# Attention and a spline FFN on one core: the copy of the FFN's constants in four parts in the second batch, and the fourth value tile projected before the first head

## The reference

```python
def reference(x, Wq, bq, Wk, bk, Wv, bv, Wo, bo, gate_cp, up_cp, down_cp):   # x: (4, 512, 512)
    xn = layernorm(x)
    # attention, 16 heads of 32
    q, k, v = (heads(xn @ W + b) for W, b in ((Wq, bq), (Wk, bk), (Wv, bv)))
    scores = q @ k.T / sqrt(32) + slope[h] * distance        # causal mask
    attention = merge(softmax(scores) @ v) @ Wo + bo
    # FFN, 512 -> 2048 -> 512; its weights are made from control points
    gate_w, up_w, down_w = (spline_reconstruct(cp) for cp in (gate_cp, up_cp, down_cp))
    ffn = (silu(xn @ gate_w.T) * (xn @ up_w.T)) @ down_w.T
    return x + attention + ffn
```

## Time and profile before

| | |
|---|---|
| Median of three executions | 844.9 us |
| The profiled execution: its time | 845.87 us |
| Its span (first to last instruction) | 844.1 us |
| Mean granted clock of TensorE | 0.912 of full speed |
| PE busy | 703.6 us (83%) |
| DVE / ACT / POOL busy | 505.1 / 439.5 / 354.6 us |
| DMA moved | 109.79 MB |

### The profile page before, as it was taken

The page is one execution under the profiler, slowest core; times in us unless marked ns, Lnnn a source line. Parts: engine busy times, 40 slices in busy tenths (PEclk is TensorE's granted clock), DMA queues, the critical chain, the costliest instruction groups (busy, mean ns, idle before and its releaser), DMA issues. The chain is left out here.

```text
span 844.1 us, 14059 instructions
## 1 busy us (share of the span) xinstructions
PE 703.6 (83%) x4884; PEld 558.1 (66%) x4884; DVE 505.1 (60%) x1273; ACT 439.5 (52%) x961; POOL 354.6 (42%) x207
## 2 busy tenths in 40 slices
PE   5677879889789898798898684169895999999997
PEld 4566657667567676576776563147684888888886
DVE  5286687779968888877798767185341321221212
ACT  4267566677748776666778751135441233233221
POOL 2343363445535444634455435145223334434434
PEclk9879689999989999899899798569997999999999
DMA  7982564454585336644545917664617545434401
GB/s 252 207 205 37 101 92 153 58 88 75 114 202 76 50 69 134 92 153 58 89 73 124 319 74 246 230 212 136 184 23 228 174 148 175 140 92 138 133 1 50
DMA packets 53024, 109.79 MB, mean 130 GB/s; under 512 B 6361, under 2 KB 6617, under 8 KB 51417
## 3 DMA queue, kind: packets, MB, share of 16 engines
q1 hardware_dynamic: 52808, 108.82, 51.6%
q10 hardware_dynamic: 144, 0.07, 0.0%
HBM read 59.32 MB, written 25.17 MB: 100 GB/s over the span
## 5 line engine op out<-in xcount | busy, mean ns | idle before, releaser
L988 POOL TENSOR_TENSOR work<-work 128x1280 f16<-128x1280 f32 x64 | 168.4, 2630 | 228.3 <-DVE work L714 228.1
L901 ACT ACTIVATE work<-work,neg_max 128x128 f32<-128x128 f32 (+3 forms) x256 | 142.2, 564 | 105.5 <-DVE neg_max L706 104.7
L706 DVE CUSTOM_DVE_ANT_0 work<-bank,dist 128x128 f32<-128x128 f32 (+3 forms) x256 | 115.4, 487 | 82.5 <-PE bank L513 68.2
L1476 POOL TENSOR_TENSOR in_lo<-inner,in_hi 128x512 fp32r<-128x512 f32 x64 | 84.0, 1313 | 180.5 <-ACT in_hi L1379 180.5
L1430 DVE TENSOR_TENSOR inner<-bank,silu 128x512 f32<-128x512 f32 x64 | 44.1, 689 | 135.7 <-ACT silu L1373 122.4
L910 ACT COPY work<-bank 128x768 f16<-128x768 f16 (+1 forms) x128 | 110.3, 909 | 28.5 <-PE bank L527 27.2
L527 PE MATMUL bank<-ident,work 128*128 128x128 f16 x1280 | 109.9, 231 | 10.3 <-DVE work L721 8.5
L513 PE MATMUL bank<-k_stack,q_stack 96*128 96x256 f32 (+2 forms) x256 | 81.6, 397 | 41.5 <-issue 22.5
L1379 ACT CAST in_hi<-inner 128x512 fp32r<-128x512 f32 x64 | 39.8, 621 | 146.4 <-PE bank L1318 137.6
L527 PEld LDWEIGHTS bank<-ident,work 128*128 128x128 f16 x1280 | 78.6, 103 | 50.4 <-issue 33.2
L1316 PE MATMUL bank<-w_room,in_hi 128*128 128x512 f32 x256 | 100.9, 394 | 0.4 <-POOL in_lo L1476 0.4
(11 more groups left out here) (101 smaller groups left out, 1429.0 us busy)
## 6 DMA issues: line engine op xcount, KB each, us to landing
q_stack<-parts SPq DMA_DIRECT2D x48, 256.0 KB, 5.6
k_stack<-parts SPq DMA_DIRECT2D x48, 256.0 KB, 5.6
z<-xt_scratch SPq DMA_DIRECT2D x128, 88.0 KB
x_in<-x SPq DMA_DIRECT2D x32, 256.0 KB, 5.7
xt_scratch<-xt_room SPq DMA_DIRECT2D x8, 1024.0 KB, 6.8
xt_room<-xt_scratch SPq DMA_DIRECT2D x6, 1024.0 KB, 8.2
factor<-c_basis SPq DMA_DIRECT2D x5, 1024.0 KB, 9.7
taps<-windows SPq DMA_DIRECT2D x5, 1024.0 KB, 11.6
```

The lines of the kernel that those rows point to most:

```text
L706: dve.tensor_tensor_reduce(probs[:, s % 2, OFF[i]:OFF[i] + n], score_bank[i % 2][:, 0:n], dist[:, S - n:S], -slope(s), 3.4e38, ALU.add, AL ...
L901: e = act.activation(tile, tile, ACT.Exp, bias=neg_max[:, s % 2, i:i + 1], scale=-1.0, accum_out=row_sum[:, s % 4, i:i + 1])
L988: pool.tensor_tensor(probs16[:, s % 2, 1, :], probs[:, s % 2, :], probs16[:, s % 2, 0, :], ALU.subtract).then_inc(lo_ready, 1)
L1476: pool.tensor_tensor(in_lo[:, k % 2, :], inner[:, k % 2, :], in_hi[:, k % 2, :].bitcast(F32), ALU.subtract).then_inc(il_ready, 1)
```

## The change

The copy of the constants becomes four DMAs of 32 rows each. `lay_out(sp, part)` issues one of them, and part 0 the zeros as well. They are issued in the round b = 1 of SP's loop, behind `stack(0, 3)`, `stack(1, 0)`, `stack(1, 1)` and `stack(1, 2)`. The fourth value tile is projected right behind the third, in front of step 0, and DVE takes all four tiles there; in the list `PJ_FIRST`, `("v", 3)` and `("q", 1)` change places.

```diff
-            sp.wait_ge(bases_st, 16)
+            sp.wait_ge(bases_st, 64)
...
-        def lay_out(sp):
-            sp.dma_start(bases_d, c_bases[:, 0:BM_COLS + BD_COLS]).then_inc(bases_st, 16)
+        def lay_out(sp, part):
+            rows = slice(part * P // 4, (part + 1) * P // 4)
+            sp.dma_start(bases_d[rows], c_bases[rows, 0:BM_COLS + BD_COLS]).then_inc(bases_st, 16)
+            if part:
+                return
...
-PJ_FIRST = [("x", t) for t in range(QT)] + [("q", 0), ("k", 0), ("v", 0), ("v", 1), ("v", 2), ("q", 1), ("v", 3),
+PJ_FIRST = [("x", t) for t in range(QT)] + [("q", 0), ("k", 0), ("v", 0), ("v", 1), ("v", 2), ("v", 3), ("q", 1),
...
-            for t in range(3):
+            for t in range(QT):
                 project_v(0, t)
             for s in range(HALF):
                 step(0, s, False)
-                if s == 0:
-                    project_v(0, 3)
...
-                if not later(b) and s in (0, 1):
-                    v_take(b, s + 2)
...
-            for t in range(2):
+            for t in range(QT):
                 v_take(0, t)
...
             stack(0, 0)
             store_xt(0)
-
-            lay_out(sp)
             stack(0, 1)
             stack(0, 2)
             for b in range(1, B):
                 for t in range(QT):
                     load_x(b, t)
                 stack(b - 1, 3)
+                if b == 1:
+                    lay_out(sp, 0)
...
                 stack(b, 0)
+                if b == 1:
+                    lay_out(sp, 1)
                 stack(b, 1)
+                if b == 1:
+                    lay_out(sp, 2)
                 store_sum(b - 1, 0)
                 store_sum(b - 1, 1)
                 stack(b, 2)
+                if b == 1:
+                    lay_out(sp, 3)
                 store_sum(b - 1, 2)
                 store_sum(b - 1, 3)
```

## The result

| | before | changed |
|---|---|---|
| Median of 22 executions each, us | 845.37 (840.85 to 849.22) | 841.87 (839.2 to 845.22) |
| Ratio to before, 95% interval | | 0.9961 (0.9947 to 0.9975) |
| Span of the profiled execution, us | 844.1 | 838.2 |
| Mean granted clock there | 0.912 | 0.926 |

The change saves 0.39% of the time, 3.3 us with an interval from 2.1 to 4.5. The forecast was 1.5 us. The two profiled executions lie 5.9 us apart, more than the medians, so a difference between their spans is read step by step and not as a whole: 0.2 us of the 5.9 lie in front of the first scores, 3.9 between these and step 4, and 1.8 behind step 4. That last stretch takes 772.5 to 777.2 us in the traces of this case (e6 aside), and for one and the same kernel 777.2 in e1 and 772.7 in r2.

The account below looks back on a forecast made before the run. A chain through all engines, not one engine, was taken to bound the first 70 us. Terms -2.7 (value tile) and +1.2 (part 3), others 0, gave -1.5 us: median 844.9 to 843.4, 8-in-10 range 840.8 to 847.1.

Parts of the forecast that it names:

- Step 0 stays, the value tile costs nothing in front of it: Before the first scores: the tile's 2.75 us of matmuls fit in PE's 6.23 us idle time; start stays 37.47, cost 0.
- The high part moves by 2.7: Step 1, head 0: bias 2.05 us earlier plus 0.60 for the take, carried through POOL and key DMAs to step 4.
- The rival that ACT stands just behind in the chain: Start of the kernel: ACT's unmoved work holds the chain, nothing is won, part 3 only adds; 846.1 us, chance 0.13.
- The rival of the clock: Step 0: shorter idle time keeps PE at 2.4 GHz, 1.4 us more comes through; 842.0 us, chance 0.15.
- Part 3 costs 1.2: Batch 1, ahead of the last two sums' stores: batch 2's input loads go 2.2 us later; cost 0 to 2.2, middle taken.
- the slow landing of batch 1's loads: Batch 2's input loads, issued in batch 1, landed after 4.5 and 4.8 us, leaving DVE no slack; cause not shown.
- The row of batch 3: The same input loads a batch later: landing after 2.7 and 3.0 us, 2.2 us of slack, so part 3 would cost nothing.
- The copy leaves the start: 0 by itself: First 53 us: the copy holds 8.7 us of the queue, but nobody waits for it, so removal alone is worth 0.
- the two edits belong together: Query DMAs of chunk 1: issued at 50.2 they would stand behind the copy, so the 2.7 us gain needs the queue free.
- Part 0, 1, 2: 0 each: Three quarters of the copy behind key stacks: each takes 2.2 us of queue where nothing waits, cost 0 each.
- The rule of the Trainium skill on DMA sizes: Copy parts of 32 rows, 736 KB: if a third slower, part 3 holds the queue 2.9 us, sum 0.7 us worse, 844.1.
- The slower rival: Batch 1, steps 0 and 8: parts 1 and 3 slow the keys ahead, 3.4 us each; 850.2 us, chance 0.07.

Follow-up runs that it names:

- e6: Changed kernel with the whole copy as one DMA behind stack(1, 2), where part 3 stood, and nothing in the other three places; ratio to before 1.0054.
- e1: Changed kernel with the copy put back as one DMA in its old place, so only the value tile is moved; ratio to before 0.9976.
- r2: Repeat of e1 (value tile moved, copy whole in its old place) on one chip with the changed kernel; ratio to before 0.9948.
- r1: The changed kernel measured again, unaltered, on one chip with the repeat of the value tile alone; ratio to before 0.9960.
- e9: Changed kernel with VectorE's takes of the third and fourth value tiles back in steps 0 and 1; one execution, 841.78 us.
- e4: Changed kernel with the whole copy as one DMA behind stack(1, 0), and nothing in the other three places; ratio to before 0.9962.
- e2: Changed kernel with the value tile and its takes put back in their old place, so only the copy is moved, in four parts; ratio to before 1.0005.
- e7: Changed kernel with 15 further matmuls, their result overwritten, filling PE's idle time before the first scores; ratio to before 0.9955.
- e11: Changed kernel with the copy as one DMA in its old place and 15 filling matmuls before step 0; ratio to before 0.9938.

## Why the prediction was right, and where it was not

The direction, the range (840.8 to 847.1) and the forecast that it stays within 0.5% (0.39% measured) held, and the chain through the first 67 us is the one that was described. The size was off, 1.5 foreseen and 3.3 measured, and half of the difference lies in part 3. (The forecast's own range should read 842.2 to 844.4: 844.9 - 2.7 + 2.2 is 844.4.) Step by step:

- **Step 0 stays, the value tile costs nothing in front of it.** Right: first scores at 37.27, the idle time 3.54 (3.5 foreseen), landing times unchanged.
- **The high part moves by 2.7.** Right, once the clock is set aside: where the low clock lies over all of step 0, as before, the distance to it is 7.68 to 7.69 instead of 10.44 (e1, e6, r1), 2.75, and to step 4 26.63 to 26.65 instead of 29.51, 2.87. DVE's splits hold the bias back as foreseen; the take's share is 0.5 to 0.6 (e9), 0.6 foreseen. The rival that ACT stands just behind in the chain is refuted: from the high part to step 4 it is 18.9 to 19.1 us in all 13 traces.
- **The rival of the clock** came in by half. I gave it 0.15 as a matter of all or nothing. What happened is a matter of where the fall lies: sometimes over the whole of step 0, sometimes only from 1 us into it and for half as long. What counts for the chain is only the stretch up to the second pair of scores, since DVE works without a pause from there to the high part: that stretch takes 3.1 us where the clock is low all through it (e1, e6, r1), 2.07 in the changed kernel and 1.7 with the gap filled. In the changed kernel's trace this gave 1.0 us beyond the 2.87, in r2 0.8, in e1, e4, e6 and r1 nothing. But e2, with the value tile in its old place, won 0.86 against before as well. The two traces of the old order have a mean distance to step 4 of 29.08 and the six of the new one without filling (e9 aside) one of 26.33. The difference, 2.75, is close to the 2.87 of the tile alone. So the clock is not shown to be part of what the medians differ by.
- **Part 3 costs 1.2.** Mechanism right, size too large: 0.64 in the changed kernel and 0.63 in e7, 0 in r1, e2 and e9, all with part 3 in its place. SP's wait grew by 1.7 and not 2.2, and the slow landing of batch 1's loads, which I could not explain and which stays unexplained, went away wherever the copy or a part of it stood in front of the stores: 2.6 to 4.1 us in e2, 4.5 to 5.2 before. The row of batch 3 was the better one, and I took the middle.
- **The copy leaves the start: 0 by itself.** Right (e2: 1.0005). But "the two edits belong together" was wrong: the value tile alone gives the whole gain (r2, 0.9948, beside the changed kernel's 0.9960 in r1), even with the query DMAs issued as early as they can be (e11). I took the copy's landing for the end of its hold on the queue. The query DMAs were issued 2.5 us before that landing in e1 and 4.6 before it in e11, and landed after their usual time or sooner.
- **Part 0, 1, 2: 0 each.** Right; the keys ahead of the four parts land 6.4 to 6.7 us after the last issue.
- **The rule of the Trainium skill on DMA sizes** ("DMA: Bandwidth & Descriptors", "Rules for kernel authors") asks for 128 partitions and at least 1 MiB, and the prediction tried out a part a third slower. SP's wait grew by 1.7 for a part of 736 KB and by 8.6 for the whole of 2944 KB with its zeros (e6, 10.7 against 2.1). A part costs less than a quarter of the whole, so the measurement shows no such loss here.
- **The slow clock after a wait.** In the Trainium skill, "TensorE: Matmul & The Clock Gate", section "HAM oscillation — how this bites in real kernels", waits on DMAs between groups of matmuls bring the slow clock back each time. The trace agrees, with 0.69 over the first 5.5 us of step 0 in the changed kernel and 1.00 in every filled run. Filling the wait is worth 0.6 to 1.6 us of the path, since DVE becomes the limit.
- **The slower rival** (the parts slow the keys ahead of them): no landing was late.

The sum with the measured terms: -2.87 for the tile and +0.3 for part 3 (the mean of its five traces), thus -2.6 against -1.5 foreseen. Of the difference, 0.9 is part 3 and 0.2 the tile. The measured 3.3 lies 0.7 beyond this sum and within its interval, 2.1 to 4.5; whether the clock, in step 0 or later, gives any of that 0.7 is open.

## What to carry to other kernels

Look for independent work of the right length to put into the wait for a transfer that a later step needs anyway; it pays what it frees in the later step's chain, here 2.87 us, of which 0.5 to 0.6 is VectorE's take and the rest the 2.75 us of matmuls, as far as VectorE's own work lets it through. Whether it saves the array's clock too changes from execution to execution. Count how much of the wait is left: what remained here, 3.5 us, still took the clock down, and filling it as well, even with work that is thrown away, was worth more than moving the copy. A DMA that nobody waits for is moved only when it has been seen in someone's way; the place to avoid is ahead of stores on whose landing a load hangs.

## What was not expected of the hardware

Transfers issued while a copy from memory to memory had not landed were not delayed by it: in e1 the copy landed at 54.2 and query DMAs issued at 51.69 to 53.0 landed within 4.3 to 6.2 us, no later than elsewhere; in e11 it landed at 54.3, and query DMAs issued at 49.67 to 51.0 landed within 4.5 to 5.6. And the point at which the granted clock falls after the same idle time varies between executions: in four traces with the value tile moved and no filling (e1, e6, r1 and the changed kernel) it fell between 1.0 us before and 1.2 us after the first scores, and PE reached step 1 after 6.20, 6.15, 6.16 and 5.04 us.
